# Dense 64-wide routing with match-and-replace, a shared expert behind the slot numbers, uneven slot-row loads, and half of the final sums on TensorE

## What is computed

```python
B, T, M, D, G, H = 2, 1024, 256, 128, 4, 4          # 16 query heads, 4 key heads
x = layernorm(x + attention(x))                      # rope, causal softmax
E, K, F, G, KG, SCALE = 64, 6, 96, 8, 4, 2.5         # 64 experts in 8 groups
CAP = 48                                             # tokens an expert takes
scores   = sigmoid(x @ gate_w)
scores_b = scores + bias
group    = sum of the 2 best scores_b of each of the 8 groups; the 4 best groups stay
topk_ids = the 6 best scores_b in these groups; topk_w = their scores / their sum * 2.5
pos      = rank of (token, expert) among the expert's tokens; dropped if pos >= CAP
y        = sum over the 6 of topk_w * (silu(x @ w_gate[e]) * (x @ w_up[e])) @ w_down[e]
shared   = (silu(x @ ws_gate) * (x @ ws_up)) @ ws_down
x = layernorm(x + y + shared)
```

## Time and profile before

| | |
|---|---|
| median of 3 runs | 1194.2 us (1193.83 to 1195.28) |
| the profiled execution | 1194.67 us, its span 1192.9 us |
| instructions | 16811 |
| busy share PE, DVE, ACT, POOL | 86%, 58%, 44%, 33% |
| attention stage | 0 to 1022 us |
| last tile's tail, to the first load of `srow` | 1022 to 1057 us |
| expert stage | 1057 to 1152 us |
| final stage | 1152 to 1193 us |

### The profile page before, as it was taken

One profiled execution on the slowest core, in us unless ns is written; L12 is line 12 of the kernel. 1 busy time (PEld: TensorE's weight loads), 2 busy tenths in 40 slices (PEclk: granted clock), 3 DMA queues, 4 the chain that ended last, 5 costly groups with the idle time before them and its releaser, 6 DMA issues.

```text
span 1192.9 us, 16811 instructions
## 1 busy us (share of the span) xinstructions
PE 1030.1 (86%) x5440; PEld 749.9 (63%) x5440; DVE 689.9 (58%) x1725; ACT 524.0 (44%) x1162; POOL 392.0 (33%) x413
## 2 busy tenths in 40 slices
PE   4789999999999999987889999999999998638810
PEld 3676667777777767666666677777777675424500
DVE  3547575556576775646575755565767756323316
ACT  2434454545454553532344545454545544123302
POOL 3111333533434242022313335233342411025632
PEclk8899999999999999988899999999999999869855
DMA  9300100000000000000000000000000084976565
GB/s 304 96 18 6 46 30 16 20 10 1 23 5 22 5 1 20 5 15 11 20 5 20 19 10 15 10 2 19 5 15 5 1 193 104 243 209 111 57 159 228
DMA packets 64436, 62.88 MB, mean 53 GB/s; under 512 B 10116, under 2 KB 61294, under 8 KB 64352
## 3 DMA queue, kind: packets, MB, share of 16 engines
q1 hardware_dynamic: 50976, 51.00, 15.1%
q0 software_dynamic: 9216, 6.36, 3.8%
q10 hardware_dynamic: 4160, 4.46, 1.2%
HBM read 39.98 MB, written 33.03 MB: 61 GB/s over the span
## 4 chain that ended last, share of the span: by engine, by line
PE 63%; DVE 16%; issue 7%; DMA 7%; POOL 4%; ACT 3%; POOLq 0%; ACTq 0%; SPq 0%; DVEq 0%
PE o_ps L919 17%; PE s_ps L895 13%; PE ring L870 10%; PE ring L908 9%; PE ring L933 8%; DMA sums<-erow,goal_u 5%; DVE neg_max L1085 3%; PE ring L876 2%; DVE q_sin L1069 1%; DVE q_cos L1067 1%; POOL slot_rows L673 1%; DVE sig L1141 1%; PE s_ps L898 1%; POOL q_rot L661 1%; PE ring L948 1%
## 5 line engine op out<-in xcount | busy, mean ns | idle before, releaser
L919 PE MATMUL o_ps<-pt,v_sb 128*128 128x512 f32 x576 | 295.2, 595 | 5.6 <-DVE ot L1113 4.7
L766 ACT ACTIVATE pt<-ring 128x512 f32<-128x512 f32 x288 | 170.9, 594 | 256.2 <-PE ring L908 256.0
L758 ACT ACTIVATE probs<-s_ps,neg_max 128x128 f32<-128x128 f32 (+7 forms) x256 | 189.6, 741 | 205.6 <-DVE neg_max L1085 200.4
L1085 DVE TENSOR_REDUCE neg_max<-s_ps 128x1 f32<-128x128 f32 (+7 forms) x256 | 190.8, 749 | 67.3 <-PE s_ps L898 66.8
L908 PE MATMUL ring<-ident,probs 128*128 128x128 f32 x1152 | 176.8, 276 | 12.4 <-ACT probs L758 8.1
L908 PEld LDWEIGHTS ring<-ident,probs 128*128 128x128 f32 x1152 | 129.6, 142 | 61.5 <-issue 59.6
L895 PE MATMUL s_ps<-kt_hi,qt_hi 128*128 128x512 f32 (+3 forms) x384 | 165.3, 430 | 2.4 <-ACT probs L758 1.4
L661 POOL TENSOR_TENSOR q_rot<-q_cos,q_sin 128x256 f32<-128x256 f32 x80 | 65.4, 817 | 244.0 <-DVE q_sin L1069 240.8
L673 POOL DMA_INDIRECT slot_rows<-row,slot_u x96 | 96.5, 1005 | 136.0 <-DVE slot_u L1219 111.6
L895 PE MATMUL s_ps<-kt_lo,qt_hi 128*128 128x512 f32 (+3 forms) x384 | 133.9, 349 | 0.0
L895 PE MATMUL s_ps<-kt_hi,qt_lo 128*128 128x512 f32 (+3 forms) x384 | 133.9, 349 | 0.0
(11 more groups left out here) (162 smaller groups left out, 1492.4 us busy)
## 6 DMA issues: line engine op xcount, KB each, us to landing
fsum<-sums SPq DMA_DIRECT2D x16, 512.0 KB, 10.3
sums<-blank SPq DMA_DIRECT2D x16, 384.0 KB, 2.4
wexp<-in_L_ffn_w_gate_dram SPq DMA_DIRECT2D x32, 192.0 KB, 5.8
wexp<-in_L_ffn_w_up_dram SPq DMA_DIRECT2D x32, 192.0 KB, 6.1
wexp<-in_L_ffn_w_down_dram SPq DMA_DIRECT2D x32, 192.0 KB, 8.0
slot_rows<-blank SPq DMA_DIRECT2D x1, 4352.0 KB, 22.7
srow<-slot_rows ACTq DMA_DIRECT2D x4, 1088.0 KB, 9.7
x_sb<-in_L_attn_x_dram SPq DMA_DIRECT2D x16, 128.0 KB, 2.1
```

Source lines behind the costliest of these rows:

```text
L758: act.activation(probs[:, u % 2, h, 0:blocks(u) * P], s_ps[:, n % 2, score_cols(n)], ACT.Exp, bias=neg_max[:, n % 8:n % 8 + 1], accum_out= ...
L766: reader(act.activation(pt[:, n % PTB, :], bank(s), ACT.Copy), s)
L919: pe.matmul(o_ps[:, :], v_sb[:, j, g * D:(g + 1) * D], pt[:, n % PTB, :], start=(j == 0), stop=(j == blocks(u) - 1)).then_inc(pv_done, 1)
L1085: dve.tensor_reduce(neg_max[:, n % 8:n % 8 + 1], s_ps[:, n % 2, score_cols(n)], AX_X, ALU.max, negate=True).then_inc(max_ready, 1)
```

## The change

Five things change together.

1. Routing. Instead of indices and one-hot rows of 6 x 64, DVE replaces the best values by a marker (`match_replace`) and compares 64-wide rows with the marker. The weights are kept as a row of 64, so a token row in `slot_rows` grows from 272 to 324 floats. Slot numbers come from `max` over 64 numbers `slots_left` minus the count.
2. The last two elementwise operations of the shared expert are a step of their own, `shared`. In the table it stands at `rtr`; for tile 15 alone `shared`, `ht` and `sd` stand behind `place`.
3. `srow` is loaded in chunks of 2, 6, 8 and 16 pairs, not four of 8. SP loads weights 24 to 27 no longer when the last `pv` is done but, with 28 to 31, after `attention_left` and the first two chunks.
4. `outproj` waits for each quarter of `ot` by itself.
5. The final stage has 8 chunks. In chunks 0, 2, 4 and 6 PE adds the four tables with float32 matmuls against the identity into PSUM; DVE adds in the others.

```diff
-SLOT_CHUNKS = 4
-PER_CHUNK = PAIRS // SLOT_CHUNKS
+SLOT_CUTS = (0, 2, 8, 16, PAIRS)
-FINAL = 4
+FINAL = 8
-W_AT, S_AT, T_AT, ROW = M, M + K, M + 2 * K, M + 16
+W_AT, T_AT, ROW = M, M + E, M + E + 4
+    (("shared",), -1, (9, 9, 9, 9)),
...
-    seq += [(s, p) for s in ("outproj", "norm", "x1t", "rtr")] + [("pick", p, 0), ("ht", p), ("pick", p, 1), ("sd", p)]
-    seq += [("pick", p, n) for n in range(2, 8)] + [("count", p), ("place", p)]
+    seq += [(s, p) for s in ("outproj", "norm", "x1t", "rtr")] + [("pick", p, n) for n in range(8)]
+    seq += [(s, p) for s in ("count", "place", "shared", "ht", "sd")]
...
-                    for n in range(homes_in(w_hi, w_lo), HOMES):
+                    for n in range(homes_in(w_hi, w_lo), homes_in(w_hi, w_lo, kt_hi, kt_lo, qt_hi, qt_lo, probs)):
...
-                        if n == homes_in(w_hi, w_lo, kt_hi, kt_lo, qt_hi, qt_lo, probs):
-                            sp.wait_ge(pv_done, PT_ALL)
...
-            for n in range(HOMES, PAIRS):
-                sp.wait_ge(dn_ready, n - HOMES + 1)
+            sp.wait_ge(attention_left, 1)
+            for g in range(2):
+                sp.wait_ge(srow_loaded[g], 16)
+            for n in range(homes_in(w_hi, w_lo, kt_hi, kt_lo, qt_hi, qt_lo, probs), PAIRS):
+                used(sp, dn_ready, n - HOMES + 1)
                 load_pair(n)
...
-                    pe.wait_ge(o_ready, G * (i + 1))
                     for h in range(G * H):
+                        if h % H == 0:
+                            pe.wait_ge(o_ready, G * i + h // H + 1)
...
+            pe.wait_ge(erow_ready, PAIRS)
+            pe.wait_ge(hid_t_ready, PAIRS)
+            for c in range(0, FINAL, 2):
+                pe.wait_ge(fsum_loaded[c], 16 * TABLES)
+                for a in range(TABLES):
+                    ins = pe.matmul(sum_rows(c), ident[:, :], fsum[:, c, a, :], start=(a == 0), stop=(a == TABLES - 1))
+                ins.then_inc(fsum_added, 1)
...
-                    after(dve.max_index(group_at[:, :], group_top[:, :], group[:, :]))
-                    later(dve.tensor_copy(group_atf[:, :], group_at[:, :]))
+                    later(dve.match_replace(group_left[:, :], group_top[:, :], group[:, :], GONE))
                 if kind == "pick" and part == 3:
-                    after(dve.tensor_tensor(kept4[:, :, :], each(iota_e[:, 0:EG], KG),
-                                            wide(group_atf[:, 0:KG], EG), ALU.is_equal))
-                    later(dve.tensor_reduce(kept[:, :], kept4[:, :, :], AX_X, ALU.add))
+                    later(dve.tensor_scalar(barred[:, :], group_left[:, 0:EG], GONE, NEG, ALU.not_equal, ALU.mult))
...
-                    after(dve.max_index(top_at[:, :], top8[:, :], open_[:, :]))
-                    later(dve.tensor_copy(top_atf[:, :], top_at[:, :]))
+                    later(dve.match_replace(left[:, :], top8[:, :], open_[:, :], GONE))
                 if kind == "pick" and part == 6:
-                    after(dve.tensor_tensor(onehot[:, :, :], wide(iota_e[:, :], K),
-                                            each(top_atf[:, 0:K], E), ALU.is_equal))
                     if i >= 1:
                         dve.wait_ge(count_ready, i)
                     with nc.allow_low_precision("zeros and ones"):
-                        dve.tensor_reduce(chose[:, :], onehot[:, :, :].rearrange("p k e -> p e k"), AX_X, ALU.add
+                        dve.tensor_scalar(chose[:, :], left[:, 0:E], GONE, None, ALU.is_equal
                                           ).then_inc(chose_ready, 1)
...
+            for c in range(1, FINAL, 2):
+                dve.wait_ge(fsum_loaded[c], 16 * TABLES)
+                for a in range(1, TABLES):
+                    add(dve.tensor_tensor(fsum[:, c, 0, :], fsum[:, c, 0, :], fsum[:, c, a, :], ALU.add))
+                    if c > 1 and a <= 2:
+                        shift(c - 4 + a)
+                dve.wait_ge(fsum_added, c // 2 + 1)
+                spread(c - 1)
+                spread(c)
```

More of the change, by code:

```diff
@@ L32 @@
 HOMES = 28
[L33 to L34 removed]
+SLOT_CUTS = (0, 2, 8, 16, PAIRS)
+SLOT_CHUNKS = len(SLOT_CUTS) - 1
+CHUNK_AT = {n: g for g, n in enumerate(SLOT_CUTS[:-1])}
 EB = 4
@@ L1140, in _ @@
                     after(dve.tensor_scalar(sig[:, :], sig[:, :], 1.0, None, ALU.add))
-                    after(dve.reciprocal(sig[:, :], sig[:, :]))
-                    after(dve.tensor_tensor(hid[:, :], bank(s)[:, E:E + F], sig[:, E:], ALU.mult))
-                    reader(dve.tensor_tensor(hid[:, :], bank(s)[:, E + F:E + 2 * F], hid[:, :], ALU.mult), s)
+                    later(dve.reciprocal(sig[:, 0:E], sig[:, 0:E]))
+                if kind == "shared":
+                    rtr = ("rtr", s[1])
+                    after(dve.reciprocal(sig[:, E:], sig[:, E:]))
+                    after(dve.tensor_tensor(hid[:, :], bank(rtr)[:, E:E + F], sig[:, E:], ALU.mult))
+                    reader(dve.tensor_tensor(hid[:, :], bank(rtr)[:, E + F:E + 2 * F], hid[:, :], ALU.mult), rtr)
                 if kind == "pick":
@@ L1201, in _ @@
                     dve.wait_ge(count_ready, s[1] + 1)
-                    reader(dve.tensor_tensor(onehot_s[:, :, :], onehot[:, :, :], wide(bank(s)[:, 0:E], K), ALU.mult), s)
+                    dve.scalar_tensor_tensor(fits[:, :], bank(s)[:, 0:E], float(CAP), chose[:, :], ALU.is_lt, ALU.mult)
+                    reader(dve.tensor_tensor(ahead[:, :], slots_left[:, :], bank(s)[:, 0:E], ALU.subtract), s)
                 if kind == "sd":
@@ L1232, in slots_of @@
             def slots_of(g):
-                pairs = slice(g * PER_CHUNK, (g + 1) * PER_CHUNK)
+                a, b = SLOT_CUTS[g:g + 2]
+                flat = srow[:, :, :].rearrange("p n r -> p (n r)")
                 dve.wait_ge(srow_loaded[g], 16)
-                step(dve.tensor_tensor(mine[:, :, :], srow[:, pairs, S_AT:S_AT + K], each(slot_at[:, pairs], K),
-                                       ALU.is_equal))
-                step(dve.tensor_tensor(mine[:, :, :], mine[:, :, :], srow[:, pairs, W_AT:W_AT + K], ALU.mult))
-                step(dve.tensor_reduce(slot_w[:, pairs], mine[:, :, :], AX_X, ALU.add))
-                step(dve.tensor_scalar(goal[:, :], srow[:, pairs, T_AT], spare[:, 0:1], None, ALU.min))
-                step(dve.tensor_tensor(goal_u[:, pairs], goal[:, :], row_base[:, pairs], ALU.add))
+                for e in range(2):
+                    half, first = slice(e * HALF, (e + 1) * HALF), a * ROW + W_AT + 2 * a + e
+                    dve.tensor_copy(slot_w[half, a:b], flat[half, first:first + (b - a - 1) * (ROW + 2) + 1:ROW + 2])
+                step(dve.scalar_tensor_tensor(goal_u[:, a:b], srow[:, a:b, T_AT], spare[:, 0:1], row_base[:, a:b],
+                                              ALU.min, ALU.add))
                 dve.tensor_copy(dve_cell[:, :], spare[:, :]).then_inc(slots_known, 1)
```

112 lines of the change are left out of this document (50 added, 62 removed).

## The result

The changed kernel takes 1158.7 us (median of 4 runs, 1157.38 to 1159.86) against 1194.74 beside it (4 runs, 1193.83 to 1195.41): a ratio of 0.9705, with a 95% interval from 0.9693 to 0.9718, 36 us less.

A forecast was written before the change was run, and what follows sets the result against it. Bound by PE (63% of the chain) in attention, DVE in the tail and final stage, POOL's adding DMAs in the expert stage. Attention -9, experts' start -1, final stage -5 make -15 from 1194.67: 1179 us, range 1169 to 1189.

The forecast's parts named there:

- The attention term: Attention stage: less DVE routing work shortens PE's waits and low-clock time, -9 us, bounds -3 and -15.
- Together 8.8: Attention stage: PE's waits fall by 3.6 us for `chose`, 1.2 for the bank, 2 for `probs`, 2 before `outproj`.
- What a shorter wait leads to is often the next wait, so I keep two thirds: Attention stage: of the 8.8 us of shorter PE waits only 6 us count as gain.
- The bound of -15: Attention stage: largest gain, if all four listed rows of PE waits go (17.9 us), less what cannot.
- The clock, 3: Attention stage, 450 to 600 us: fewer waits halve part of 21 us at the low clock; PE wins 3.5, taken as 3.
- The tail's -6.9: Tile 15: `outproj` wait of 0.87 us goes and the routing chain takes 5.8 us, not 11.8; -5.5 to -8.
- The experts' start: Adding DMAs: 7.4 us earlier start, 0.6 left at the 7th pair as loads slow the rounds; taken as -1 us.
- The final stage's -5: Final stage: eight chunks with PE sharing the additions save 6 us, taken as -5; bounds 0 and -6.5.
- That DVE's relief doesn't reach PE: Rival, attention stage: `probs` waits are chain length, not queue, so only 3 us gained; 1185 us, chance 0.16.
- That the head start is kept: Rival, experts' start: adding DMAs hold pace beside the loads, so the 7.4 us stay; 1172.5 us, chance 0.12.
- PE late in the final stage: Rival, final stage: PE stays at the low clock throughout and ends its additions at 1184.9; total 1184 us, chance 0.08.
- The slower case: Rival, experts' start: adding DMAs take 17 us a round for two rounds, eating all gains; 1197 us, chance 0.05.

The follow-up runs named there:

- routing alone: Changed kernel with only the dense routing kept; tile 15's order, chunks, weight loads, `outproj` and final stage as before: 1164.02 us, 0.9746.
- The runs with the filler: Changed kernel plus five unread DVE products per routing: late in tiles 0 to 14, 1188.48 us; early, 1177.69; late only where PE is full, 1160.28.
- weights early: Changed kernel with weights of pairs 24 to 27 loaded as before, once the last `pv` is done: 1157.5 us, 0.9709.
- parts joined, equal: Changed kernel with tile 15's order, SP's weight loads and four equal `srow` chunks as before; routing, `outproj` by quarters and final stage stay changed: 1155.71 us, 0.9685.
- weights behind store: Changed kernel with weights of pairs 24 to 27 issued directly behind the last store of `z_sb`: 1158.71 us, 0.9703.
- equal chunks: Changed kernel with `srow` loaded in four equal chunks of 8 pairs: 1158.78 us, 0.971.

## Why the prediction was wrong, step by step

**The attention term failed: -9, and -15 at most, where the stage gave 30.6 us, 0.9 of it the wait before the last `outproj`.** Three steps of it were at fault.

"Together 8.8": PE's waits behind DVE's queue fell by 17.3 us (3.6 for `chose`, 3.4 and 3.0 for `probs`, 3.4 and 2.7 for `ot`, 1.2 for the bank). The first and the last were foreseen to 0.1. But the prediction tied the relief to waits behind routing by name. In a full queue everything that stands behind routing comes sooner, the copies to `ot` and the scaling of `probs` as well: 5.7 us that no term had. PE's idle time fell by 20.0 in all. With the routing alone 2.8 of the 3.4 us before `outproj` are still there, so these are the quarters'.

"What a shorter wait leads to is often the next wait, so I keep two thirds": in tiles 2, 3 and 8 to 11 no next wait came; the time fell by 21.3 us for 22.4 us of DVE. The runs with the filler show it both ways: 29.8 to 34.6 us back for 48.7 us of DVE in all tiles, and nothing in tiles 1 to 14 for 17.3 us where PE is full. The bound of -15, all four rows, was no bound.

The clock, 3: the low level fell from 30.7 to 17.1 us, worth half of the difference, 6.8, at most, and 5.9 by the time in which PE worked during it (28.3 and 16.6 us). The 21 us counted were those of 150 us of the stage alone. 20.0 and 5.9 leave 4.7 us by which PE's busy time fell for no reason that a row names. 4.4 of them are in tiles 1 to 7 and 10 to 15, which had the high clock throughout in both profiles, so the clock is not it; pauses inside matmuls whose ends are modelled are one way, which nothing here tests.

**The rest held.** The tail's -6.9: -7.1, and 0.9 more ahead of its first matmul. The store hidden: right. The experts' start, a head start of 7.4 us of which 0.6 is left, taken as -1: from `outproj` to the 7th adding DMA it is 65.9 before and 65.05 after, -0.9, and -1.8 with the 0.87 before `outproj`, which the 7.4 contain. Its working, three rounds at 9.5, 8.5 and 6.5, came out at 8.9, 8.7 and 8.4. The final stage's -5: -5.7. "At the high level 3.4" for four additions was 3.70, and the first chunk 5.40. The row that the 3.4 names gives 3.70 itself: five records in 2.31 us are 0.92 us for two, not 0.86. The 4.6 us for a round of two pairs from the 7th on is 4.8 by the same trace (59.4 us for 25 pairs); the sum uses it only as a comparison.

The Trainium skill (DMA: Bandwidth & Descriptors, "Queues, rings and completion order") says that an engine goes round-robin between the queue rows that have work. The trace agrees so far: with the store on ScalarE's queue, 0.13 MB of that queue and 0.93 MB of SP's moved from 1020 to 1024 us. Yet the queue of its own won the store nothing (7.4 us, 7.1 on SP's queue): its first packet ran 5.1 us after its issue, where the first of `srow` in the kernel after ran 1.0 us after its own. Why it started so late no run here shows.

**The rivals.** That DVE's relief doesn't reach PE had 0.16 and was wrong the other way. That the head start is kept is excluded by the 26.0 us. PE late in the final stage: it waited for loads. The slower case, rounds of 17 us: they were 8.9 at most. None of the cases was "the attention term is three times as large", so the chances had no room for what happened.

**What the tail's head start turned into.** From the issue of the `srow` loads to the 7th adding DMA, by the bytes of `srow` and weights loaded in that time:

```
kernel                  MB     us
before                  6.8   31.2
weights early           7.7   32.6
parts joined, equal     7.7   32.9
routing alone           7.7   33.3
weights behind store    8.2   34.4
equal chunks           10.0   37.3
after                  10.0   37.5
```

About 2 us for each MB in these seven profiles, whichever queue the store took and whatever the chunks. Moving the weights moves this time between two columns.

## What to carry to other kernels

A sum of visible waits bounds nothing from above where an engine's queue is full while the bottleneck pauses. Cut the stage into its repeating units, and for each read how long the bottleneck stands idle. In the units where PE was idle for 2.7 us or more a microsecond of DVE was worth a microsecond; where it was idle 0.7 us or less, nothing; in between (tiles 5 and 13, idle 1.4 us) less than half. DVE's own busy share doesn't tell them apart: in the first four heads it was 77 to 85% in tiles 2, 3 and 8 to 11 and 84 to 89% in tiles 4, 6, 7, 12 and 14, which gave nothing. A head start into a stage that is limited by bytes is given back, and a step moved to ease one engine's queue has to be walked through every other queue it issues into, here POOL's.
